# Cross-attention in fp32r pairs on one Trainium2 core: scores through a precomputed Wq_h^T K_h, and seven-product block multiplication for both large products

## The chip, the cores and the metric

The kernel runs on one core of a Trainium2 chip. The metric is the device time of one execution in microseconds. The engines have short names in the profile: PE is the matrix engine and PEld its weight load, DVE the vector engine, ACT the scalar engine, POOL the GpSimd engine, SP the engine that issues all DMAs here (SPq is its queue).

## The reference

The reference is one cross-attention layer, in fp32. B = 8 batches, T = 1024 rows of x, D = 1024, 16 heads of 64, and only S = 64 context rows in a batch.

```python
a = _layer_norm(audio_kv, ln_gamma, ln_beta)          # (8, 64, 1024)
Q = (hidden_states @ Wq.T)  ...  K = (a @ Wk.T)  ...  V = (a @ Wv.T)     # split in 16 heads
scores = jnp.einsum('bhtd,bhsd->bhts', Q, K) * scale
scores = jnp.where(mask, scores, -inf)
attn = jax.nn.softmax(scores, axis=-1)
out = jnp.einsum('bhts,bhsd->bhtd', attn, V)
out = out @ Wo.T                                       # heads side by side again
return hidden_states + jnp.tanh(gate) * out
```

The host only lays out the inputs (x also transposed, weights transposed).

## The kernel before

**Three products for one.** Every operand of a large product is held as two fp32r parts: hi is the operand copied to fp32r (ACT does it), lo is the operand minus hi (DVE or POOL does it). One block product is then three matmuls of 128x128 by 128x512 into one PSUM bank: lo by hi, hi by lo, hi by hi. These are lines L938, L939 and L940 (`product`), whatever the stage, so the three lines carry nearly all of PE's time.

**Stages.** The program has three stages, one after the other.

1. Context: layer norm of the 512 context rows (all batches), 32 transposes (L950), K and V for all batches: 64 block products each. K (scaled) and V (hi and lo) go to scratch tensors in DRAM.
2. Attention, `all_batches` over 8 batches of 16 units. A unit is one pair of heads (128 columns of Q) by 512 rows of x: 8 block products for Q (`q_part`), a copy of Q to SBUF (ACT, L703), the scores as plain fp32 matmuls against `k_diag` (`scores`, L1019; K of two heads on the diagonal of a 128x128 block, so that scores of two heads come out side by side), mask and maximum and shift (DVE), exponential (ACT, L727), row sums (DVE), normalising (POOL, L576), four transposes of the probabilities (`transpose_p`, L1031), their split (ACT L735, DVE L844), one block product against `v_diag` (`values`), and a copy (ACT, L743) that goes to `o_t_scratch` in DRAM. The stages of different units overlap by lags of 1 to 4 units; PE's order is first half of Q, scores of the unit before, second half of Q, values of three units before, transposes of two units before:

```python
all_batches(pe, [(q_first, 0), (scores, SCORES_LAG), (q_second, 0), (values, VALUES_LAG),
                 (transpose_p, TRANSPOSE_LAG)], lambda j: out_product(0, j))
```

3. Output product, 8 batches of 28 items. Here D by D times T is already cut in 2 x 2 blocks and done by seven products (Strassen's) instead of eight: for four groups of 256 rows, seven items each, an item being 4 x 3 matmuls. POOL forms the sums of blocks of the attention output (L610), ACT (L760) and DVE (L889) split them, DVE adds each finished item with factor tanh(gate) to one, two or three quarters of x in SBUF (L920), SP stores the result. The sums of Wo's blocks are made once.

Q's product (8 block products of 512 columns a unit) is done in full, with no such saving. All loads and stores are issued by SP in program order. The attention part of ACT, DVE and POOL is idle in stage 3, and nothing of stage 3 runs in stage 2, but for a few items at the seam.

The matmuls add up as follows. 128x512: 192 for K, 192 for V, 128 units x 24 for Q, 128 x 3 for values, 8 x 28 x 12 for the output, 6528 in all. 128x128: 512 fp32 score matmuls that the profile counts as two each (1024), and 512 + 32 transposes. That is the 8096 of the page.

## Time and profile before

| | |
|---|---|
| time, median of 3 runs | 1701.82 us (1701.62 to 1704.45) |
| span of the profiled execution | 1697.8 us |
| its own time beside the span | no time of its own is listed for it; the median lies 4.0 us above the span |
| PE busy | 1669.2 us, 98% |
| DVE, ACT, POOL busy | 931.4, 541.5, 608.3 us |
| granted clock of PE | 1.000 over the whole span (2.4 GHz) |
| DMA | 212.53 MB, 125 GB/s mean |

PE's "busy" is the union of its matmuls, whose modelled ends overlap; the distance from one start to the next says more than the duration of one. The page gives shares over the whole span; the windows below give them by stage.

### The profile page before, as it was taken

To read this page: it belongs to the slowest core of one execution; us is meant where nothing else is said; L and a number is where in the kernel's file an instruction comes from. 1 tells how busy PE (TensorE), PEld (TensorE's weight loads), DVE (VectorE), ACT (ScalarE), POOL (GpSimd) and SP (SyncE) were. 2 spreads that over 40 slices of the span, in tenths; PEclk is the share of its full clock that TensorE was granted. 3 is DMA by queue.
4 is the path that set the end of the run, shared out by engine and by line. 5 is a ranking of instruction groups with operands and counts; after the bars stand their busy time and mean duration, and the time that the engine had idled before them with its cause. 6 is when DMAs were issued, how large, how long until landed. Compare 5 with 4: busy or idle time off the path is not lost.

```text
span 1697.8 us, 23996 instructions
## 1 busy us (share of the span) xinstructions
PE 1669.2 (98%) x8096; PEld 1394.7 (82%) x8096; DVE 931.4 (55%) x1436; ACT 541.5 (32%) x942; POOL 608.3 (36%) x489
## 2 busy tenths in 40 slices
PE   6999999999999999999999999899999999999999
PEld 5878888888888888888888888678888888888887
DVE  6045644444444444444444444777666666666666
ACT  3243333333333333333333333522222222222221
POOL 6345632332332332332322323743333333333331
PEclk9999999999999999999999999999999999999999
DMA  5466442222222222222222221555444455445442
GB/s 200 163 239 212 161 141 78 80 76 73 79 75 74 83 71 74 82 73 74 86 69 76 80 67 63 180 195 191 160 148 148 175 179 189 150 167 178 149 149 100
DMA packets 117166, 212.53 MB, mean 125 GB/s; under 512 B 36480, under 2 KB 36608, under 8 KB 117120
## 3 DMA queue, kind: packets, MB, share of 16 engines
q1 hardware_dynamic: 117120, 211.93, 36.6%
q8 instruction: 27, 0.44, 0.1%
q14 instruction: 19, 0.16, 0.0%
HBM read 133.24 MB, written 78.64 MB: 125 GB/s over the span
## 4 chain that ended last, share of the span: by engine, by line
PE 95%; DVE 2%; DMA 2%; issue 1%; ACT 0%; POOL 0%; SPq 0%; DVEq 0%; ACTq 0%; POOLq 0%
PE banks L938 28%; PE banks L940 28%; PE banks L939 28%; PE banks L1019 7%; PE banks L1031 3%; DMA w_stage<-o_t_scratch 0%; DVE probs L920 0%; DMA o_t<-x 0%; DMA probs<-x 0%; DVE stats L800 0%; PE banks L950 0%; DVE act_in L793 0%; DMA out<-probs 0%; DVE o_t L920 0%; DMA act_in<-ctx_x 0%
## 5 line engine op out<-in xcount | busy, mean ns | idle before, releaser
L938 PE MATMUL banks<-act_hi,w_lo 128*128 128x512 f32 x1088 | 448.1, 412 | 1.5 <-DVE probs L838 1.5
L940 PE MATMUL banks<-act_hi,w_hi 128*128 128x512 f32 x1088 | 426.2, 392 | 0.0
L939 PE MATMUL banks<-act_lo,w_hi 128*128 128x512 f32 x1088 | 425.5, 391 | 0.0
L565 POOL TENSOR_TENSOR act_lo<-act_in,act_hi 128x512 fp32r<-128x512 f32 x128 | 164.9, 1290 | 601.3 <-ACT act_hi L657 601.3
L727 ACT ACTIVATE probs<-probs 128x512 f32<-128x512 f32 x128 | 80.9, 632 | 548.8 <-DVE probs L881 548.8
L869 DVE TENSOR_TENSOR probs<-banks,mask_bias 128x512 f32<-128x512 f32 x128 | 88.7, 693 | 286.1 <-PE banks L1019 286.1
L940 PEld LDWEIGHTS banks<-act_hi,w_hi 128*128 128x128 f32 x1088 | 204.5, 188 | 45.0
L938 PEld LDWEIGHTS banks<-act_hi,w_lo 128*128 128x128 f32 x1088 | 205.5, 189 | 36.6 <-DVE probs L838 1.9
L939 PEld LDWEIGHTS banks<-act_lo,w_hi 128*128 128x128 f32 x1088 | 205.8, 189 | 35.1
L760 ACT CAST act_hi<-block_sum 128x512 fp32r<-128x512 f32 x160 | 99.3, 620 | 333.2 <-POOL block_sum L610 173.4
L938 PE MATMUL banks<-w_hi,act_lo 128*128 128x512 f32 x512 | 199.7, 390 | 3.2 <-issue 3.2
L940 PE MATMUL banks<-w_hi,act_hi 128*128 128x512 f32 x512 | 199.3, 389 | 0.0
L939 PE MATMUL banks<-w_lo,act_hi 128*128 128x512 f32 x512 | 199.2, 389 | 0.0
L889 DVE TENSOR_TENSOR act_lo<-block_sum,act_hi 128x512 fp32r<-128x512 f32 x160 | 114.6, 716 | 123.4 <-ACT act_hi L760 123.4
L938 PE MATMUL banks<-act_hi,act_lo 128*128 128x512 f32 x448 | 174.7, 390 | 2.6 <-issue 1.6
L940 PE MATMUL banks<-act_hi 128*128 128x512 f32 x448 | 174.3, 389 | 0.0
L939 PE MATMUL banks<-act_lo,act_hi 128*128 128x512 f32 x448 | 174.3, 389 | 0.0
L610 POOL TENSOR_TENSOR block_sum<-w_stage 128x512 f32<-128x512 f32 x80 | 103.4, 1293 | 196.5 <-DVE act_lo L889 194.3
L610 POOL TENSOR_TENSOR block_sum<-act_in 128x512 f32<-128x512 f32 x80 | 104.6, 1309 | 175.0 <-DVE act_lo L889 175.0
L844 DVE TENSOR_TENSOR p_lo<-banks,p_hi 128x512 fp32r<-128x512 f32 x128 | 88.5, 692 | 112.9 <-ACT p_hi L735 112.9
L1019 PEld LDWEIGHTS banks<-k_diag,q_t 128*128 128x128 f32 x1024 | 133.8, 191 | 10.4 <-ACT q_t L703 0.5
L576 POOL TENSOR_TENSOR probs<-probs,row_rec 128x512 f32<-128x512 f32 x128 | 134.4, 1050 | 6.9 <-DVE row_rec L859 6.9
(77 smaller groups left out, 2238.4 us busy)
## 6 DMA issues: line engine op xcount, KB each, us to landing
act_in<-x_t SPq DMA_DIRECT2D x128, 256.0 KB, 3.1
o_t_scratch<-o_t SPq DMA_DIRECT2D x128, 256.0 KB, 3.1
probs<-x SPq DMA_DIRECT2D x32, 512.0 KB, 3.7
w_stage<-o_t_scratch SPq DMA_DIRECT2D x8, 2048.0 KB, 9.9
out<-probs SPq DMA_DIRECT2D x32, 512.0 KB, 3.4
act_in<-o_t_scratch SPq DMA_DIRECT2D x7, 2048.0 KB, 10.1
q_t<-x SPq DMA_DIRECT2D x16, 512.0 KB, 3.3
o_t<-x SPq DMA_DIRECT2D x16, 512.0 KB, 4.3
```

The costliest lines, as they stand in the source:

```text
L565: nc.gpsimd.tensor_tensor(act_lo[:, par, c, :], act_in[:, c, :], act_hi[:, par, c, :].bitcast(F32), ALU.subtract).then_inc(act_lo_made, 1)
L576: nc.gpsimd.tensor_tensor(pr, pr, rec, ALU.mult).then_inc(probs_done, 1)
L610: nc.gpsimd.tensor_tensor(o_sum[:, n % 2], o_part(g, one), o_part(g, other), ALU.add if sign > 0 else ALU.subtract).then_inc(part_summed, 1)
L727: nc.scalar.activation(probs[:, j % 4, :], probs[:, j % 4, :], ACT.Exp).then_inc(exp_done, 1)
L760: nc.scalar.copy(ring(k)[0], src).then_inc(part_hi_made, 1)
L844: nc.vector.tensor_tensor(p_lo[:, j % 2, :], banks[:, 4 + j % 2, :], p_hi[:, j % 2, :].bitcast(F32), ALU.subtract).then_inc(p_lo_made, 1)
L869: nc.vector.tensor_tensor(grouped(j), scores, bias, ALU.add).then_inc(masked, 1)
L889: nc.vector.tensor_tensor(lo, src, hi.bitcast(F32), ALU.subtract).then_inc(part_lo_made, 1)
L938: pe.matmul(to, wl, mh, start=first, stop=False)
L939: pe.matmul(to, wh, ml, start=False, stop=False)
L940: return pe.matmul(to, wh, mh, start=False, stop=last)
L1019: m = pe.matmul(banks[:, 2 + j % 2, cols], q_t[:, j % 2, cols], k_diag[:, p, :], start=True, stop=True)
```

## The change

The computation is reordered. For every batch and head, x Wq_h^T K_h^T = x (Wq_h^T K_h^T): a 1024 x 64 matrix for each head, so for each batch one 1024 x 1024 matrix M (16 heads side by side) is made once, and the scores of all heads are one product x M. Q, `q_t` and `k_diag` no longer exist.

1. **Context stage.** K as before, but all eight banks at once. Then 16 groups (`m_pair` by `v_tile`): a group makes M for all batches, for 128 rows of it and 8 heads, by 4 pairs x 6 matmuls whose contraction is 64 rows (a head), head 0 of a pair on partitions 0 to 63 and head 1 on 64 to 127, into different banks, one after the other in turn; in between come the matmuls of V (12 a group, two groups late). ACT and DVE copy M to one of three 2 MB buffers, SP stores it in DRAM (`store_m`: 1024 runs of 2 KB; batches are 4 MiB apart).
2. **Main stage: 224 steps in one pattern.** A round is 512 rows of x by the whole D, in seven products (steps) of 512 x 512 x 512, Winograd's form, where later products are added in PSUM to earlier ones. A step is two items (`item`, g = 0, 1) of 4 x 3 matmuls each. 16 rounds make the scores (16 x 7 = 112 steps), 16 rounds the output (112 steps). In a score round the first product starts with one more matmul for each g that adds the mask (L1079). For each step ACT and DVE split one block sum of the left operand (128x1024, `split_a_hi`, `split_a_lo`) into a ring of two, POOL makes 4 sums a round, and the results leave PSUM as 128x1024: 4 copies by ACT and 3 additions by DVE in a score round, 7 additions by DVE in an output round (`add_out`). The right operand (`parts`: seven block sums of M, hi and lo) is made anew for each batch, that is every 14 steps: 14 splits of 128x1024 on ACT and on DVE, 4 sums of 128x2048 on DVE. For the output it is made once, in 28 pieces, during steps 106 to 117.
3. **Attention beside it.** The scores go to DRAM and come back (256 KB a unit). Each unit (a pair of heads by 512 rows, 128 in all, 8 a round) passes seven stages, one half step apart each, one unit every 1.75 half steps, beginning half a round ahead of the output round that uses it: row maximum (DVE), exponential (ACT, now eight ACTIVATEs of 64 columns, since the shift is their bias; the mask addition and the shift on DVE are gone), row sum and reciprocal (DVE), normalising (POOL), transposes (PE), split (ACT, DVE), values (PE), copy into the x buffers (ACT; no trip through DRAM any more).

tanh(gate) is folded into V. The loops over batches are written out, with no branch. The residual x is loaded into the result buffer first, as before. Counts now: 128x512 matmuls 192 (K) + 384 (M) + 192 (V) + 2688 + 32 (scores and mask) + 2688 (output) + 384 (values) = 6560; transposes 512 + 32; fp32 score matmuls none. Of the 6560, the 384 for M use 64 of the 128 rows.

The core of the diff, PE first, then SP, then ACT and DVE (lines before: -, now: +):

```diff
-        def q_part(b, j, chunks):
...
-            for c in chunks:
-                if p == 0:
-                    pe.wait_ge(act_lo_made, n * NC + c + 1)
-                cols = slice(p * P, (p + 1) * P)
-                m = product(banks[:, j % 2, :], (w_hi[:, c, cols], w_lo[:, c, cols]),
-                            (act_hi[:, blk, c, :], act_lo[:, blk, c, :]), c == 0, c == NC - 1)
-        def scores(b, j):
...
-            for t in range(TPB):
-                cols = slice(t * P, (t + 1) * P)
-                m = pe.matmul(banks[:, 2 + j % 2, cols], q_t[:, j % 2, cols], k_diag[:, p, :],
-                              start=True, stop=True)
-            m.then_inc(scores_done, 1)
...
+        for i in range(GROUPS + V_LAG):
+            v = i - V_LAG
+            for half in range(2):
+                if i < GROUPS:
+                    for p in range(2 * half, 2 * half + 2):
+                        m_pair(i, p)
+                if v >= 0:
+                    for t in range(2 * half, 2 * half + 2):
+                        last = v_tile(v, t)
+            if v >= 0 and v % 2 == 1 and v % NC != NC - 1:
+                last.then_inc(v_used, 1)
...
+        def m_pair(i, p):
...
+                pe.wait_ge(m_copied_a, pair - 1)
+                pe.wait_ge(m_copied_b, pair - 1)
+            hp = 4 * hh + p
+            for t_w, t_k in ((1, 0), (0, 1), (0, 0)):
+                for h in range(2):
+                    rr = slice(h * HEAD, (h + 1) * HEAD)
+                    m = pe.matmul(banks[:, 2 * (p % 2) + h, :], w_ring[rr, w % 6, t_w, hp * P:(hp + 1) * P],
+                                  k_parts[rr, t_k, hp, :], start=t_w == 1, stop=t_w == 0 and t_k == 0)
+            m.then_inc(m_done, 1)
...
+        def store_m(i):
+            wait_group(i)
+            sp.dma_start(m_rows(i, 0, B), m_stage[i % 3][:]).then_inc(m_stored[i % 3], 16)
...
+        def item(s, g):
+            n, k = s // 7, s % 7
+            rnd = s // 14
+            if g == 0:
+                pe.wait_ge(a_lo_made, s + 1)
...
+            to = banks[:, 4 + g, :] if k in ON_F else banks[:, 2 * (n % 2) + g, :]
+            opens = k in ON_F[::2] or k == P1
+            if k == P1 and n < ROUNDS:
+                pe.matmul(to, ones_row[:], mask_mov[:].rearrange("p h s -> p (h s)"), start=True, stop=False,
+                          skip_group_check=True)
+                opens = False
+            for c in range(HC):
+                last = three(to, [a_ring[:, s % 2, t, c, g, :] for t in range(2)],
+                             [parts[:, k, t, c, :] for t in range(2)], opens and c == 0, c == HC - 1, True)
+            last.then_inc(item_done, 1)
...
+        for z in range(2 * STEPS):
+            item(z // 2, z % 2)
+            for u in units(z, VALUES):
+                values(u)
+            for u in units(z, TURN):
+                transpose_p(u)
...
+    MAX, EXP, SUM, TURN, SPLIT, VALUES, EVAC = 0, 1, 2, 3, 4, 5, 6
+    def unit_slot(u):
+        return 14 * (ROUNDS + u // 8 - 1) + 14 * (u % 8) // 8 - 7
...
+        def split_a_hi(s):
...
+            wait(act, item_done, 2 * (s - 1))
...
+            nc.scalar.copy(a_ring[:, s % 2, 0], a_source(n, k)).then_inc(a_hi_made, 1)
...
+        def exponential(u):
+            act.wait_ge(max_done, u + 1)
+            for g in range(8):
+                cols = slice(g * S, (g + 1) * S)
+                last = nc.scalar.activation(probs[:, u % 4, cols], probs[:, u % 4, cols], ACT.Exp,
+                                            bias=neg_max[:, u % 2, g:g + 1])
+            last.then_inc(exp_done, 1)
-            nc.scalar.activation(probs[:, j % 4, :], probs[:, j % 4, :], ACT.Exp).then_inc(exp_done, 1)
...
+        for s in range(STEPS):
+            if s + 1 < STEPS:
+                split_a_hi(s + 1)
+            if s > 0:
+                copy_out((s - 1) // 7, (s - 1) % 7)
+            if s < 104:
+                for rnd, q in refills(s):
+                    split_b_hi(rnd, q)
+            for z in (2 * s, 2 * s + 1):
+                for u in units(z, SPLIT):
+                    split_p_hi(u)
+                for u in units(z, EVAC):
+                    copy_o(u)
+                for u in units(z, EXP):
+                    exponential(u)
+            if s >= 104:
+                for rnd, q in refills(s):
+                    split_b_hi(rnd, q)
...
+        for s in range(STEPS):
+            rnd = s // 14 + 1
+            if s > 0:
+                add_out((s - 1) // 7, (s - 1) % 7)
+            if s + 1 < STEPS:
+                split_a_lo(s + 1)
+            if s < 104:
+                refill(s)
+            for z in (2 * s, 2 * s + 1):
+                for u in units(z, SUM):
+                    sum_rows(u)
+                for u in units(z, MAX):
+                    row_max(u)
+                for u in units(z, SPLIT):
+                    split_p_lo(u)
+            if s >= 104:
+                refill(s)
+            if s % 14 == 9 and rnd < B:
+                make_mask(rnd)
...
+        def add_out(n, k):
...
+            nc.vector.tensor_tensor(c_out[:, q], bank_pair(n, k), c_out[:, q], ALU.add).then_inc(added, 1)
+        def split_b_lo(rnd, q):
...
+            nc.vector.tensor_tensor(parts[:, k, 1, c:c + 2, :], b_raw[:, B_HOME[k], c:c + 2, :],
+                                    parts[:, k, 0, c:c + 2, :].bitcast(F32), ALU.subtract).then_inc(b_lo_made, 1)
```

What this does to the order of instructions, on the engines on which the prediction rests. First PE, at a unit's scores in the attention stage of the kernel before, and behind it the end of a unit:

```order
L939 MATMUL banks<-act_lo,w_hi 128x512
L940 MATMUL banks<-act_hi,w_hi 128x512
L1019 MATMUL banks<-k_diag,q_t 128x128 x4
L938 MATMUL banks<-act_hi,w_lo 128x512
L939 MATMUL banks<-act_lo,w_hi 128x512
```

The four fp32 matmuls L1019 stand between two halves of Q. In the changed kernel PE's order in an output round is this (12 matmuls of a step's item end with the first row; `p_parts` are the split probabilities, `a_ring` and `parts` the two operands of the step):

```order
L968 MATMUL banks<-parts,a_ring 128x512
L966 MATMUL banks<-p_parts,v_diag 128x512 [waits o_made,p_lo_made]
L967 MATMUL banks<-p_parts,v_diag 128x512
L968 MATMUL banks<-p_parts,v_diag 128x512
L1092 MATMUL banks<-ident,probs 128x128 [waits p_lo_made,probs_done]
L1092 MATMUL banks<-ident,probs 128x128 x3
L966 MATMUL banks<-parts,a_ring 128x512
```

No L1019 is left; values and transposes moved from between halves of Q to between items of the output product. Second, PE in a group of the context stage, where M and V alternate:

```order
L968 MATMUL banks<-w_ring,a_parts 128x512
L1002 MATMUL banks<-k_parts,w_ring 128x512 [waits m_copied_b,m_copied_a]
L1002 MATMUL banks<-k_parts,w_ring 128x512 x5
L1002 MATMUL banks<-k_parts,w_ring 128x512 [waits m_copied_b,m_copied_a]
L1002 MATMUL banks<-k_parts,w_ring 128x512 x5
L966 MATMUL banks<-w_ring,a_parts 128x512
```

These twelve L1002, two pairs, are new work; each pair waits for ACT's and DVE's copies of the pair two before it. Third, ACT: a unit in the kernel before, and then nearly a step and a half of an output round now.

```order
L703 COPY q_t<-banks 128x512
L735 CAST p_hi<-banks 128x512
L657 CAST act_hi<-act_in 128x512
L743 COPY o_t<-banks 128x512
L727 ACTIVATE probs<-probs 128x512
```

```order
L697 ACTIVATE probs<-probs,neg_max 128x64 x8
L656 CAST a_ring<-xq 128x1024
L706 CAST p_parts<-banks 128x512
L714 COPY xq<-banks 128x512
L697 ACTIVATE probs<-probs,neg_max 128x64 x8
L656 CAST a_ring<-a_sum 128x1024
```

The copy of Q is gone, the exponential is in eight pieces, and the split of the next step's operand (L656) now stands behind attention work on the same engine.

## Rows read from the trace of the kernel before

**Rows 1.** The page, part 1: busy time, share of the span, instructions

```profile
PE 1669.2 (98%) x8096; PEld 1394.7 (82%) x8096; DVE 931.4 (55%) x1436; ACT 541.5 (32%) x942; POOL 608.3 (36%) x489
```

**Rows 2.** The page, part 4: shares of the chain that ended last

```profile
PE 95%; DVE 2%; DMA 2%; issue 1%; ACT 0%; POOL 0%; SPq 0%; DVEq 0%; ACTq 0%; POOLq 0%
```

**Rows 3.** Windows: us, busy by engine (instructions), PE clock, DMA share, GB/s

```profile
600.00:1050.00 450.00, 450.00 (x2340) 380.68 (x2338) 213.35 (x360) 164.44 (x300) 137.13 (x120) 1.00 0.24 76
1050.00:1080.00 30.00, 27.02 (x138) 21.66 (x137) 17.24 (x28) 11.44 (x22) 12.40 (x11) 1.00 0.21 71
1080.00:1120.00 40.00, 35.20 (x149) 27.05 (x148) 35.09 (x38) 20.02 (x36) 34.38 (x24) 1.00 0.58 198
```

**Rows 4.** Timeline of PE in the output stage, matmuls 27 places apart: start, us

```profile
1499.80 0.39 PE L938 MATMUL banks<-act_hi,act_lo 128*128 128x512 f32 x1
...
1505.92 0.39 PE L938 MATMUL banks<-act_hi,act_lo 128*128 128x512 f32 x1
```

**Rows 5.** The chain in order of time, attention stage: start, us, one unit's scores

```profile
275.82 0.89 PE banks L1019 x8
```

**Rows 6.** Timeline of PE at the start: context transposes, then K's first product

```profile
16.35 3.04 PE L950 MATMUL banks<-ident,act_in 128*128 128x128 f32 x13 [2.88 <-DVE act_in L793]
19.28 0.76 PE L938 MATMUL banks<-act_hi,w_lo 128*128 128x512 f32 x1
```

**Rows 7.** The chain at the end: last matmul, last addition

```profile
1694.21 0.24 PE banks L940
1694.48 0.75 DVE o_t L920
```

**Rows 8.** DMA issues: tensors, count, KB each, median us to landing

```profile
out<-probs SPq DMA_DIRECT2D x32, 512.0 KB, 3.4
act_in<-o_t_scratch SPq DMA_DIRECT2D x7, 2048.0 KB, 10.1
```

**Rows 9.** Windows with the DMA engines near full

```profile
75.00:80.00 5.00, 5.00 (x24) 4.14 (x23) 0.00 (x0) 0.14 (x1) 0.53 (x1) 1.00 1.04 409
...
95.00:100.00 5.00, 5.00 (x24) 4.14 (x23) 2.71 (x4) 3.15 (x3) 0.00 (x0) 1.00 0.95 354
```

**Rows 10.** Groups by line and shape: busy us, mean ns, idle before

```profile
L654 ACT CAST w_hi<-w_stage 128x1024 fp32r<-128x1024 f32 x16 | 16.6, 1049 | 20.9 <-DMA w_stage<-wk_t 15.2 <-DMA w_stage<-wq_t 5.7
L813 DVE TENSOR_TENSOR w_lo<-w_stage,w_hi 128x1024 fp32r<-128x1024 f32 x8 | 11.0, 1391 | 54.6 <-ACT w_hi L654 54.6
L920 DVE SCALAR_TENSOR_TENSOR probs<-banks,tanh_gate,probs 128x512 f32<-128x512 f32 x160 | 114.9, 743 | 7.9 <-DMA probs<-x 7.9
L853 DVE TENSOR_REDUCE row_sum<-probs 128x8 f32<-128x512 f32 x128 | 87.8, 686 | 88.6 <-ACT probs L727 88.6
L859 DVE RECIPROCAL row_rec<-row_sum 128x8 f32<-128x8 f32 x128 | 24.7, 193 | 0.0
L844 DVE TENSOR_TENSOR p_lo<-banks,p_hi 128x512 fp32r<-128x512 f32 x128 | 88.5, 692 | 112.9 <-ACT p_hi L735 112.9
L735 ACT CAST p_hi<-banks 128x512 fp32r<-128x512 f32 x128 | 75.2, 587 | 62.6 <-PE banks L1031 62.6
L727 ACT ACTIVATE probs<-probs 128x512 f32<-128x512 f32 x128 | 80.9, 632 | 548.8 <-DVE probs L881 548.8
L662 ACT ACTIVATE tanh_gate<-gate_s 128x1 f32<-128x1 f32 x1 | 0.2, 198 | 0.0
L610 POOL TENSOR_TENSOR block_sum<-act_in 128x512 f32<-128x512 f32 x80 | 104.6, 1309 | 175.0 <-DVE act_lo L889 175.0
L576 POOL TENSOR_TENSOR probs<-probs,row_rec 128x512 f32<-128x512 f32 x128 | 134.4, 1050 | 6.9 <-DVE row_rec L859 6.9
```

**Rows 11.** Timeline of DVE: the shortest kind of split, and the longest

```profile
1080.90 0.69 DVE L889 TENSOR_TENSOR act_lo<-block_sum,act_hi 128x512 fp32r<-128x512 f32 x1 [0.32 <-ACT act_hi L760]
...
1086.19 1.77 DVE L889 TENSOR_TENSOR act_lo<-act_in,act_hi 128x512 fp32r<-128x512 f32 x1
```

**Rows 12.** The page, part 3: the queue that brings instructions: packets, MB, share

```profile
q8 instruction: 27, 0.44, 0.1%
```

1473 lines of the change are left out of this document (752 added, 721 removed), and 7 rows, old and new, of the table PRODUCTS.

## Prediction

> **What bounds the kernel now.** I read the page first. PE is busy for 98% of the span [rows 1], and the chain that ended last is PE's own work for 95% [rows 2], so the time is PE's work laid end to end, and the change has to be priced on PE. The busy time of the other engines is not in the sum as long as each stays below PE stage by stage; that is the second question. The clock needs no term: the windows show it at 1.00, the upper of its two levels, 2.4 GHz, with PE working without a break [rows 3].
>
> The price of a matmul I take from starts, not from durations (0.39 us, which overlap). In the output stage 27 matmuls of 128x512 start within 1505.92 - 1499.80 = 6.12 us, so one costs 0.2267 us [rows 4]. In the attention stage 2340 instructions fill 450 us without idle time [rows 3]. A unit has 27 of 128x512, 8 score passes and 4 transposes, 39 in all, so there are 60 units and one takes 7.50 us. 27 x 0.2267 = 6.12 leaves 1.38, of which 0.89 are the scores [rows 5] and 0.49 the four transposes and the seams.
>
> I test this on the kernel before: 19.3 to the first product of K [rows 6], 6528 x 0.2267 = 1479.9, 128 x 1.38 = 176.6, the other 16 context transposes 1.8, PE's idle time at the change of stage 3.0 + 4.8 [rows 3], 3.6 from the start of the last matmul to the end [rows 7]. Together 1689, 9 us under the span of 1697.8 (0.5%). So the method is good to half a per cent, and errs low.
>
> **The change, part by part.**
>
> *Start.* The first product of K now comes behind all 32 context transposes instead of behind 16. Thirteen took 3.04 us at the start, 0.23 each [rows 6]; 16 more cost 3.7: 23.0.
>
> *K.* 192 x 0.2267 = 43.5, as before.
>
> *M and V.* 576 matmuls; one after the other that is 130.6. Two things can move it. M's 384 work on 64 of the 128 rows, neighbours on different halves. No row of before shows such matmuls. From above each costs a full 0.2267 (the streamed columns are the same 512); from below two neighbours share one slot, 192 slots fewer, 43.5 us less, 87.1 for the stage. But the stage also moves about 45 MB: 33.6 MB of M, 6 of weights, the rest V, sums of Wo, first blocks of x. With the DMA engines full the rows show 409 and 354 GB/s [rows 9], so 110 to 127 us whatever PE does. So a gain on PE is mostly taken back by the stores of M. I take 125, from DMA's slower full rate, a little under PE's serial 131; ends 110 and 162 (the latter is 16 stores of 2 MB one after the other at the 10.1 of the only 2048 KB row [rows 8]).
>
> The Trainium skill ("TensorE: Matmul & The Clock Gate", Part 3, Packing small matmuls) says that small matmuls whose operands lie in different row groups run side by side, 3.07 times as fast for four of 32 rows. By it the 87.1 would be PE's own bound; no run so far shows it. My sum stays at 125 by the DMA rows either way.
>
> *Scores.* 112 steps x 24 + 32 mask matmuls = 2720 x 0.2267 = 616.6. In the place of this stood Q (3072) and the fp32 scores: here the change gives 352 x 0.2267 + 128 x 0.89 = 194 us, of which M takes back 87 at its serial price. That difference is nearly the whole gain: seven products instead of eight on D x D, and no fp32 passes.
>
> *Output and attention.* 2688 + 384 = 3072 x 0.2267 = 696.4, and 128 x 0.49 = 62.7 for transposes: 759.1. PE's count here is unchanged; only its neighbours are new.
>
> *Are the other engines hidden?* A batch of scores (14 steps) takes PE 340 x 0.2267 = 77.1. ACT has 28 splits and 8 copies of 128x1024 at 1.05: 37.8. DVE has 28 splits at 1.39, 4 sums twice that size, 6 additions at 2 x 0.743: 38.9 + 11.1 + 8.9 = 58.9 (76%). POOL has 8 sums at 2 x 1.31: 21 [rows 10]. An output round (7 steps) takes PE 168 x 0.2267 + 8 x (0.68 + 0.49) = 47.5. DVE: 7 x (1.49 + 1.39) + 8 x (0.686 + 0.686 + 0.193 + 0.692) = 38.2 (80%). POOL 10.5 + 8.4 = 19. ACT: 7 x 1.05 + 8 x (0.587 for each of the two PSUM copies) + 64 short exponentials at e each = 16.7 + 64 e. The rows have 0.198 for one column and 0.632 for 512; 64 columns on the line between are 0.25, so 32.7 (69%) [rows 10]. All hidden, at nothing, and if the cover went: ACT alone would set the round above e = 0.48.
>
> The latency also fits. The operand of step s + 1 may be split when product s - 1 is done (ring of two). In a score step ACT needs 1.05 and then DVE 1.39; DVE may first have an addition of 1.49, beside ACT. That is 2.9 of 5.44 us. In an output step the two splits come first in the loop, and attention's waits stand behind them, so PE gets a late operand only if an engine falls behind by over 3 us. What presses on DVE is POOL: a 128x512 split takes 0.69, and 1.77 at worst [rows 11]. POOL is busy 27% to 40% of the time here, so I add nothing in steady state.
>
> *Two seams.* Between context and scores DVE owes a copy of M, two splits of M's first block sum, a sum of 2.8 and the first operand, 0.7 + 2.8 + 2.8 + 1.4 = 7.7, behind 1.05 of ACT, 8.7 in all, against 5.4 of PE (24 matmuls of V): 3.3 late. In steps 0, 1 and 4 DVE has three splits and a sum, 6.95 against 5.44, 4.5 more; less what other steps absorb: 7 in all. In steps 106 to 117 the 28 pieces of Wo add 28 x 0.69 = 19.3 to DVE, 1.6 a step, so 7.1 against 6.8, four us late, and SP's loads of pieces wait for splits: 5.
>
> *End.* The last addition is 128x1024, 1.5, and a 512 KB store 3.4 [rows 8, 10]: 5.
>
> Sum: 23.0 + 43.5 + 125 + 616.6 + 759.1 + 7 + 5 + 5 = 1584, and 5 for what the same method left out above (half of the 9, since one seam of two is new work already counted): 1589. The median stood 4.0 over the profiled span before, so **1593**.
>
> **The rivals.**
>
> *M goes side by side and its stores keep up.* For it: the windows at 409 GB/s. Against it: those are short and mostly loads, and here SP must first wait for each group's copies. The stage takes 110, and the first seam vanishes in part: 1593 - 15 - 7 = 1571 to 1578. 17%.
>
> *A helper or a store sets the pace somewhere.* Either M's stores run one after the other (162 instead of 125: 1630), or ACT and DVE, with attention's waits between their splits in strict order, hold each of 112 output steps up by 0.3: 1627. For it: DVE at 80% with a split that can take 2.5 times its price. Against it: three buffers for M, and three us of slack. 18%.
>
> *Slower: M's stores.* A store writes 2 KB runs to eight places 4 MiB apart, as no store before does. If that ran at half the rate of the 2048 KB row, 20.2 a group, the stage would take 323 instead of 125: 1791. It decides above (125 + 109) / 16 = 14.6 us a store. Against it: neighbouring partitions lie 4 KB apart, as in the loads of that row. 4%. The skill ("DMA: Bandwidth & Descriptors", Latency and other measured facts) speaks against the change here: it gives 103 GB/s for copies whose partitions lie 4 MiB apart against 214 with padding, by which 2.1 MB would take 20 us; its case has that distance between partitions, ours between runs of one partition.
>
> *Slower: eight short exponentials.* If 64 columns cost nearly what 512 do, 0.632, ACT's round is 57.1 against 47.5, 16 x 9.6 = 154 late: 1747. It decides above e = 0.59. 1%.
>
> That the change has no effect would need new stalls of just 109 us, 1%; loops written out mean more code to load, but 27 packets bring half a megabyte now [rows 12], and the products of V, straight code too, run without a gap [rows 9].
>
> **How the numbers follow.** Forecast 59%: 1593, its own range 1578 to 1612. The rivals 17, 18, 4, 1 and 1%. Low end 1567 takes in the first rival; high end 1633 both forms of the second; outside are the slower cases and the tails, some 17%. A change of 0.2% (3.4 us) is about what can be told from none. Faster 94%, same 1%, slower 5%.
>
> **What would show it.** No fp32 matmul; PE's distance 0.227 in all stages; 5.4 to 5.5 us from step to step in the scores, 6.8 in the output; PE busy above 96%. M's pairs: two starts within a few ns would mean side by side, then DMA near full for 110 us and PE waiting for copies that wait for stores. The 64-column ACTIVATE near 0.25. I am wrong if PE waits for `a_lo_made` in most output steps, or if a 2 MB store lands over 14 us after its issue.

## The result, and the profile after

The changed kernel takes 1643.08 us (median of 4 runs, 1641.88 to 1643.65), beside 1701.72 for the kernel before on the same chip: 58.6 us less; the ratio is 0.9648, 95% interval 0.9636 to 0.9660 (the two medians alone give 0.9655). The prediction was 1593.0 with 1567 to 1633 as its range: the direction was right, the gain was half of what was forecast, and the time lies 10 us above the range. The profiled execution has a span of 1640.1, so the time to explain is 1640.1 against the sum of 1589. One execution of e6 below took 5479.87 us, which nothing on record explains; it is a slow run and left out of e6's time.

The page of the changed kernel, parts 1, 4 and 6 (they answer to [rows 1, 2, 8]):

```profile
PE 1554.1 (95%) x7104; PEld 1254.7 (77%) x7104; DVE 1173.1 (72%) x1216; ACT 860.6 (52%) x1822; POOL 536.4 (33%) x294
...
PE 69%; DVE 14%; issue 6%; DMA 6%; ACT 4%; POOL 0%; SPq 0%; ACTq 0%; DVEq 0%; POOLq 0%
...
m_scratch<-m_stage SPq DMA_DIRECT2D x14, 2048.0 KB, 15.6
```

The count of matmuls is the forecast one. But the chain is no longer one engine's: of 95% PE it has become 69%, and DVE holds 14%. A chain of that kind says that PE waits now and then, and the windows say where: M and V, the first seam (the change from one stage to the next, with its first round), score rounds, second seam, output rounds (columns as in [rows 3]).

```profile
63.00:180.00 117.00, 105.06 (x578) 69.61 (x576) 49.47 (x74) 53.34 (x85) 33.79 (x15) 0.97 1.02 353
180.00:290.00 110.00, 92.66 (x368) 74.26 (x368) 87.86 (x57) 47.81 (x51) 31.07 (x11) 0.89 0.56 190
290.00:768.00 478.00, 460.86 (x2015) 376.45 (x2014) 366.93 (x233) 209.88 (x213) 138.28 (x47) 1.00 0.46 157
768.00:932.00 164.00, 144.83 (x643) 117.03 (x642) 118.22 (x147) 107.94 (x261) 50.44 (x32) 0.96 0.53 164
932.00:1595.00 663.00, 660.26 (x3106) 542.56 (x3105) 486.83 (x631) 416.43 (x1182) 247.89 (x166) 1.00 0.43 135
```

PE's order is known, so the starts of its matmuls give the length of each of the 224 steps. This table is worked out from them (us; a step of 24 matmuls at the price of [rows 4] is 5.44, the first of a score round 5.89, an output round 47.5, a score round with attention beside it 47.9):

```
round  step 0     1     2     3     4     5     6    sum
  0     14.84  8.15  5.61  9.25  8.31  5.44  5.44   57.0
  7      5.89  5.44  5.46  5.57  7.19  5.58  5.44   40.6
  8      5.89  5.44  5.44  5.44  6.79  5.59  5.44   40.0
 14      5.89  5.44  5.44  5.44  5.44  8.47  7.28   43.4
 15      7.07  6.60 13.87  8.32  6.61  7.05  8.24   57.8
 16     11.37  7.29 12.09  7.43  6.61  9.91  7.26   62.0
 19      6.61  6.60  7.11  6.61  6.59  6.97  7.28   47.8
```

Against the prediction's sum, term by term:

| Term | Predicted | Measured |
|---|---|---|
| Start to K's first product | 23.0 | 19.6 |
| K | 43.5 | 43.7 |
| M and V | 125 | 116.3 (63.35 to 179.63) |
| First seam (gap before step 0 and round 0, over 38.5) | 7 | 25.3 |
| Score rounds 1 to 13, over 38.5 each | 0 | 23.6 |
| Rounds 14 to 16 (163.1), over 38.5 + 2.8 + 47.9 + 47.5 | 5 | 26.4 |
| Rounds 17 to 31 (704.1), over 699.5 | 0 | 4.6 |
| Last matmul to the end | 5 | 5.0 |

The 2.8 are what attention already gives PE in round 14: three units' transposes and two units' values. The differences add up to 18.3 + 23.6 + 21.4 + 4.6 - 3.4 - 8.7 + 0.2 = 56.0; the sum of 1589 held 5 for what the method leaves out, and 51.0 are left of the 51.1 by which the span is over it. Three places hold nearly all of the loss, each about a third.

**The score rounds.** One step of nearly each round is late. DVE beside that step, in an odd round (start, us; the step that begins at 434.19 has the late operand, and the table books the wait to the step before it, so DVE's row that ends there is the one to start from, and one reads upwards):

```profile
413.71 4.13 DVE L862 TENSOR_TENSOR parts<-b_raw,parts 128x1024 fp32r<-128x1024 f32 x2 [0.63 <-ACT parts L680]
417.94 2.29 DVE L883 TENSOR_TENSOR b_raw<-b_raw 128x2048 f32<-128x2048 f32 x1
...
421.41 1.23 DVE L862 TENSOR_TENSOR parts<-b_raw,parts 128x1024 fp32r<-128x1024 f32 x1
422.55 2.64 DVE L844 TENSOR_SCALAR mask_mov<-mask_u 1x512 fp32r<-1x512 uint8 x1
...
426.25 1.21 DVE L862 TENSOR_TENSOR parts<-b_raw,parts 128x1024 fp32r<-128x1024 f32 x1
427.57 4.31 DVE L883 TENSOR_TENSOR b_raw<-b_raw 128x2048 f32<-128x2048 f32 x1
431.80 1.21 DVE L905 TENSOR_TENSOR c_out<-banks,c_out 128x1024 f32<-128x1024 f32 x1
432.93 1.21 DVE L849 TENSOR_TENSOR a_ring<-xq,a_ring 128x1024 fp32r<-128x1024 f32 x1
...
443.07 2.35 DVE L862 TENSOR_TENSOR parts<-b_raw,parts 128x1024 fp32r<-128x1024 f32 x2
```

POOL in the same stretch, and PE's late step:

```profile
413.22 2.40 POOL L552 TENSOR_TENSOR a_sum<-xq 128x1024 f32<-128x1024 f32 x1 [3.51 <-DVE a_ring L849]
421.54 3.37 POOL L552 TENSOR_TENSOR a_sum<-xq 128x1024 f32<-128x1024 f32 x1 [5.92 <-DVE a_ring L849]
426.47 3.26 POOL L552 TENSOR_TENSOR a_sum<-a_sum,xq 128x1024 f32<-128x1024 f32 x1 [1.55 <-DVE a_ring L849]
```

```profile
434.19 0.50 PE L966 MATMUL banks<-parts,a_ring 128*128 128x512 f32 x1 [1.58 <-DVE a_ring L849]
```

The same work has two prices. The 128x2048 sum takes 2.29 us at 417.94, with POOL idle, and 4.31 at 427.57, beside POOL's sum of 426.47. Two splits take 2.35 at 443.07 and 4.13 at 413.71, beside POOL's of 413.22. The mask row, one partition of 512, takes 2.64, and 0.41 where POOL is idle. In three steps DVE loses 2.0 + 1.8 + 2.2 = 6 us, and PE's step is 1.75 late (7.19 for 5.44).

The rows show how the price comes about: of two such instructions the one that starts second waits until the first has ended. POOL's sum that starts at 421.54 finds DVE's split of 421.41 at work; the split keeps its 1.23, and POOL's sum, 2.40 where it starts alone, takes 3.37 and ends 2.27 after the split. DVE's mask row then starts at 422.55 in the middle of POOL's sum, which ends at 424.91, and itself ends 0.28 behind it. In the same way POOL's sum of 426.47 waits for DVE's split of 426.25, and DVE's sum of 427.57 waits for POOL's, which ends at 429.73, and ends 2.15 later. This holds for all of DVE's instructions of these kinds between 290 and 768 us: those that start within a sum of POOL's end 1.08 (split), 2.15 (sum) or 0.28 us (mask row) after it, within 0.01, and those that start before POOL's take their short time.

**The first seam** is a chain of transfers. In order of time:

```profile
161.15 15.54 DMA m_scratch<-m_stage
...
176.71 13.95 DMA xq<-x_t
...
190.78 2.39 POOL a_sum L552
...
193.19 1.06 ACT a_ring L656
...
194.28 2.46 DVE a_ring L849
...
201.24 0.77 PE banks L966
202.01 0.43 PE banks L967
```

The second half of x has its place in a buffer that M's stage holds, so its load waits for a store, and then shares the DMA engines with the next stores. Between the last two pieces shown the chain has 4.51 us of "issue". DVE's rows have work there, the two splits of M's block sum that this step needs too, and the granted clock follows:

```profile
196.65 4.49 DVE L862 TENSOR_TENSOR parts<-b_raw,parts 128x1024 fp32r<-128x1024 f32 x2
...
218.14 6.00 DVE L862 TENSOR_TENSOR parts<-b_raw,parts 128x1024 fp32r<-128x1024 f32 x2 [0.63 <-ACT parts L680]
```

```profile
201.30:206.00 4.70, 4.70 (x11) 3.71 (x12) 4.65 (x4) 3.00 (x3) 1.18 (x1) 0.50 0.65 235
```

Both pairs take 2.35 with POOL idle, and PE starts 0.1 us after each of them ends: 2.1 and 3.65 us of this seam are contention with POOL as well. The matmuls after the gap are 0.43 apart, with a granted clock of 0.50: PE's clock had fallen to the lower of its two levels, 1.2 GHz, during the idle time before them. By the starts, three waits (6.8 before step 0, 5.9 before step 1, 3.7 before step 4) and 35 matmuls at the lower clock behind them, 7 us, are 23 of the 25.3.

**The second seam** has two waits. ACT and DVE in step 106, where four pieces of Wo are split with three buffers:

```profile
828.96 0.62 ACT L670 CAST parts<-wo_piece_ab 128x512 fp32r<-128x512 f32 x1 [4.01 <-DMA wo_piece_ab<-wo_t]
```

```profile
824.84 4.00 DVE L857 TENSOR_TENSOR parts<-wo_piece_ab,parts 128x512 fp32r<-128x512 f32 x2
...
847.20 1.28 DVE L857 TENSOR_TENSOR parts<-wo_piece_ab,parts 128x512 fp32r<-128x512 f32 x2
```

The fourth piece can only be loaded when the first is split (4.01 us of waiting). And two splits take 4.00 at 824.84, with POOL's normalising of 824.44 and its sum of 825.44 beside them, but 1.28 at 847.20.

### The profile page after: what moved, and what is told of

It is laid out like the page before. It is cut to its first block, busy times and chain, and to the rows that moved or that the text cites. A ratio compares the mean times of both kernels' runs of the same rounds, so it can differ in the third digit from the quotient of the medians.

```text
span 1640.1 us, 19978 instructions
## 1 busy us (share of the span) xinstructions
PE 1554.1 (95%) x7104; PEld 1254.7 (77%) x7104; DVE 1173.1 (72%) x1216; ACT 860.6 (52%) x1822; POOL 536.4 (33%) x294
## 4 chain that ended last, share of the span: by engine, by line
PE 69%; DVE 14%; issue 6%; DMA 6%; ACT 4%; POOL 0%; SPq 0%; ACTq 0%; DVEq 0%; POOLq 0%
PE banks L966 22%; PE banks L968 21%; PE banks L967 21%; DVE a_ring L849 4%; DVE parts L862 3%; PE banks L1092 3%; DVE c_out L905 2%; DMA w_raw<-wq_b 2%; ACT parts L680 1%; PE banks L1002 1%; DMA w_raw<-wv_t 1%; ACT c_out L691 1%; DMA m_scratch<-m_stage 1%; DVE mask_mov L844 1%; DVE b_raw L883 1%
## 5 line engine op out<-in xcount | busy, mean ns | idle before, releaser
L966 PE MATMUL banks<-parts,a_ring 128*128 128x512 f32 x1792 | 717.6, 400 | 30.7 <-DVE a_ring L849 18.2
L968 PE MATMUL banks<-parts,a_ring 128*128 128x512 f32 x1792 | 703.4, 393 | 0.0
L967 PE MATMUL banks<-parts,a_ring 128*128 128x512 f32 x1792 | 702.8, 392 | 0.0
L966 PEld LDWEIGHTS banks<-parts,a_ring 128*128 128x128 f32 x1792 | 339.7, 190 | 106.0 <-DVE a_ring L849 25.2
L968 PEld LDWEIGHTS banks<-parts,a_ring 128*128 128x128 f32 x1792 | 339.1, 189 | 73.5
L967 PEld LDWEIGHTS banks<-parts,a_ring 128*128 128x128 f32 x1792 | 339.9, 190 | 67.2
L697 ACT ACTIVATE probs<-probs,neg_max 128x64 f32<-128x64 f32 x1024 | 259.1, 341 | 49.2 <-DVE neg_max L910 49.2
L905 DVE TENSOR_TENSOR c_out<-banks,c_out 128x1024 f32<-128x1024 f32 x160 | 195.1, 1219 | 119.0 <-PE banks L968 114.4
L849 DVE TENSOR_TENSOR a_ring<-a_sum,a_ring 128x1024 fp32r<-128x1024 f32 x128 | 188.4, 1472 | 113.7 <-ACT a_ring L656 112.5
L656 ACT CAST a_ring<-a_sum 128x1024 fp32r<-128x1024 f32 x128 | 134.0, 1047 | 211.6 <-PE banks L968 202.3
L552 POOL TENSOR_TENSOR a_sum<-xq 128x1024 f32<-128x1024 f32 x64 | 167.8, 2622 | 210.0 <-DMA xq<-x_t 105.1
L862 DVE TENSOR_TENSOR parts<-b_raw,parts 128x1024 fp32r<-128x1024 f32 x112 | 186.1, 1676 | 29.4 <-ACT parts L680 29.0
L656 ACT CAST a_ring<-xq 128x1024 fp32r<-128x1024 f32 x96 | 100.5, 1046 | 159.6 <-PE banks L968 159.6
L680 ACT CAST parts<-b_raw 128x1024 fp32r<-128x1024 f32 x112 | 115.2, 1047 | 60.2 <-DVE b_raw L883 54.4
L849 DVE TENSOR_TENSOR a_ring<-xq,a_ring 128x1024 fp32r<-128x1024 f32 x96 | 123.9, 1291 | 2.4 <-ACT a_ring L656 2.4
## 6 DMA issues: line engine op xcount, KB each, us to landing
m_scratch<-m_stage SPq DMA_DIRECT2D x14, 2048.0 KB, 15.6
```

The source lines that it names most:

```text
L552: nc.gpsimd.tensor_tensor(a_sum[:, A_SUM[k]], one, two, op).then_inc(sum_made, 1)
L656: nc.scalar.copy(a_ring[:, s % 2, 0], a_source(n, k)).then_inc(a_hi_made, 1)
L680: nc.scalar.copy(parts[:, k, 0, c:c + 2, :], b_raw[:, B_HOME[k], c:c + 2, :]).then_inc(b_hi_made, 1)
L697: last = nc.scalar.activation(probs[:, u % 4, cols], probs[:, u % 4, cols], ACT.Exp, bias=neg_max[:, u % 2, g:g + 1])
L849: nc.vector.tensor_tensor(a_ring[:, s % 2, 1], a_source(n, k), a_ring[:, s % 2, 0].bitcast(F32), ALU.subtract).then_inc(a_lo_made, 1)
L862: nc.vector.tensor_tensor(parts[:, k, 1, c:c + 2, :], b_raw[:, B_HOME[k], c:c + 2, :], parts[:, k, 0, c:c + 2, :].bitcast(F32), ALU.subtra ...
```

## The experiments

Unless said otherwise each is the changed kernel with one edit; times are medians, with the ratio to the kernel before (1702.1 to 1702.8 beside these runs) and its interval.

**e1: DVE's order.** In the score steps the split of the next operand comes before the addition.

```diff
-                if s > 0:
+                if s > 0 and s >= 112:
                     add_out((s - 1) // 7, (s - 1) % 7)
                 if s + 1 < STEPS:
                     split_a_lo(s + 1)
+                if 0 < s < 112:
+                    add_out((s - 1) // 7, (s - 1) % 7)
```

> Edit: in the 112 score steps DVE splits the next operand before it adds the finished product to the result, not after. First theory (DVE runs late at the fifth step of a round, P7, because an addition of 1.2 us and a block sum stand ahead of the split that PE waits for): that step goes from 7.19 and 6.79 us to about 6.0 and 5.6, 14 rounds x 1.2 = 17 us, so about 1626. Rival (the late operand comes from ACT or from POOL's sum, or PE waits for the addition itself): the step stays at 7.2 and 6.8, or another step takes over the delay, 1643.

1654.69, ratio 0.9719 [0.9703, 0.9735]: 12 us slower. The late step of the even rounds is 8.01 instead of 6.79. Its rows on DVE:

```profile
391.51 4.27 DVE L883 TENSOR_TENSOR b_raw<-b_raw 128x2048 f32<-128x2048 f32 x1
395.71 3.43 DVE L849 TENSOR_TENSOR a_ring<-xq,a_ring 128x1024 fp32r<-128x1024 f32 x1
399.06 1.21 DVE L905 TENSOR_TENSOR c_out<-banks,c_out 128x1024 f32<-128x1024 f32 x1
```

In the changed kernel, in the same round, the addition comes first, beside this sum of POOL's:

```profile
390.12 1.21 DVE L905 TENSOR_TENSOR c_out<-banks,c_out 128x1024 f32<-128x1024 f32 x1
391.25 2.30 DVE L849 TENSOR_TENSOR a_ring<-xq,a_ring 128x1024 fp32r<-128x1024 f32 x1
```

```profile
388.13 4.34 POOL L552 TENSOR_TENSOR a_sum<-a_sum,xq 128x1024 f32<-128x1024 f32 x1
```

The addition, one of whose operands is in PSUM, takes 1.21 beside POOL, and only what is then left of POOL's sum falls on the split. In e1 the split, both operands in SBUF, waits out POOL's sum by itself (3.43), the addition runs after it, and PE waits 2.41 for the addition. So the order before the edit had put the work that POOL does not touch beside POOL. The theory that order alone was at fault fell.

**e2: POOL's sums made small.** After round 0 the sums take 4 of 128 columns (this leaves most of the block sums out).

```diff
-                nc.gpsimd.tensor_tensor(a_sum[:, A_SUM[k]], one, two, op).then_inc(sum_made, 1)
+                w = 4 if n > 0 else P
+                nc.gpsimd.tensor_tensor(a_sum[:, A_SUM[k], :, :, 0:w], one[:, :, :, 0:w], two[:, :, :, 0:w], op
+                                        ).then_inc(sum_made, 1)
```

> Edit: POOL's sums of blocks of the left operand cover 4 of 128 columns in every round but the first (so most of these sums is left out); all waits, splits and products stay. Theory (DVE's two-input work in SBUF nearly stands still while POOL's works, which is why the 128x2048 sum takes 4.3 instead of 2.3 us and the mask row 2.6): L883 falls to 2.3 in all calls, the mask row to 0.4, the fifth step of a round to 5.44, 14 x 1.6 = 23 us in the score rounds and some in the second seam, about 1612. Rival (DVE simply has too much work ahead of the split): L883 shortens little, the step stays above 6.5, above 1635.

1604.88, ratio 0.9430 [0.9415, 0.9446]. Every step of score rounds 1 to 13 is 5.44 (5.89 the first): 38.5 a round, as the sum had it. DVE's groups in the score rounds (lines are 2 further down here) are all at their short price:

```profile
L885 DVE TENSOR_TENSOR b_raw<-b_raw 128x2048 f32<-128x2048 f32 x24 | 55.0, 2291 | 2.4 <-DVE parts L864 0.5
L846 DVE TENSOR_SCALAR mask_mov<-mask_u 1x512 fp32r<-1x512 uint8 x6 | 2.8, 470 | 0.0
```

That was 76.6 us with a mean of 3190 ns, and 13.6 with 2261, in the changed kernel. So the loss in the score rounds goes with POOL's sums. Small sums are also ready sooner for ACT; e6 and e12, in which they come later and the loss goes too, rule that out as the cause. The output rounds take 47.4 instead of 47.8, so what they lose goes with the sums as well. But the second seam stayed, 56.6 + 58.3 for rounds 15 and 16 where it was 57.8 + 62.0.

**e3: an eighth of M stored** (the other seven batches are left out, and all rounds read the first).

```diff
-                sp.dma_start(m_rows(i, 0, B), m_stage[i % 3][:]).then_inc(m_stored[i % 3], 16)
+                sp.dma_start(m_rows(i, 0, 1), m_stage[i % 3][:, 0:1]).then_inc(m_stored[i % 3], 16)
```

> Edit: only one batch of M in eight is stored (256 KB instead of 2 MB a group), and all rounds read that one; so 7/8 of the stores of M are left out, everything else stays. Theory (the stage of M and V and the start of the scores are set by the stores of M, the DMA engines being full): the stage falls from 116 to 90 to 97 us (PE's own 87 plus waits for copies), and the delay at the first steps from 25 us to under 8; together about -40, 1603. Rival (PE waits for the copies of M by ACT and DVE, or DVE's own work makes the first steps late): the stage stays above 110 and the first round at 50 us or more, above 1630.

1625.53, ratio 0.9546 [0.9530, 0.9562]. With the DMA engines half idle the stage still takes 109.0 (116.3 before):

```profile
63.00:172.00 109.00, 104.31 (x577) 69.24 (x576) 54.23 (x76) 57.50 (x89) 37.27 (x17) 0.97 0.49 160
```

So the stores cost the stage 7 us, and PE with what it waits for the rest. They cost more behind it: round 0 fell from 57.0 to 47.8.

**e4: head by head.** A pair's three matmuls for head 0 (rows 0 to 63), then three for head 1.

```diff
-                for t_w, t_k in ((1, 0), (0, 1), (0, 0)):
-                    for h in range(2):
+                for h in range(2):
+                    for t_w, t_k in ((1, 0), (0, 1), (0, 0)):
```

> Edit: in a pair of M the three matmuls of head 0 come first and then the three of head 1, so that neighbours use the same 64 rows, instead of taking turns. Theory (matmuls on different halves of the rows run side by side, and the stage is held by its stores, so only what exceeds them costs): twelve of them take 2.7 to 3.0 instead of 1.66 us, PE's work in the stage becomes 131, the stage goes from 116 to about 131, 1658. Rival (a matmul of 64 rows is short by itself): 1.66 us again and 1643. If the stores did not hold the stage, it would be +43, 1686.

1646.39, ratio 0.9666 [0.9650, 0.9682]: no change in the stage (116.9). Twelve matmuls take the same time in both orders. This did not decide between side by side and short by itself, which needed e9.

**e5: a fourth buffer for pieces of Wo.**

```diff
-        wo_piece_in = sems("wo_piece_in", 3)
+        NP = 4
+        wo_piece_in = sems("wo_piece_in", NP)
...
-            return wo_piece_c[:, :] if pc % 3 == 2 else wo_piece_ab[:, pc % 3, :]
+            if pc % NP >= 3:
+                return wo_piece_de[:, pc % NP - 3, :]
+            return wo_piece_c[:, :] if pc % NP == 2 else wo_piece_ab[:, pc % NP, :]
```

> A fourth 2 KB slot for the pieces of Wo, so that a step that holds four pieces has no round trip of a load inside it. Theory (at the second seam the splits wait for pieces that SP may load only when a slot comes free): the two waits of ACT for pieces, 4.0 and 2.6 us, and their echo go, rounds 15 and 16 fall from 57.8 + 62.0 to some 110, the time from 1643 to 1633. Rival (the seam is DVE's own load, and its work beside POOL's): ACT waits less, DVE ends no sooner, within 2 us of 1643.

1641.38, ratio 0.9635 [0.9612, 0.9657]: not to be told from no change. Rounds 15 and 16 are 53.8 + 61.5.

**e6: POOL waits for DVE.** The first sum for the next round waits for DVE's sum of B.

```diff
+                    if 0 < n < ROUNDS:
+                        pool.wait_ge(t_made, 4 * (n // 2) + (2 if n % 2 == 0 else 4))
                     one, two, op = a_quad(n, 1, 0), a_quad(n, 1, 1), ALU.add
```

> POOL's first sum of the next round waits until DVE has made the sum of B in that stretch (two of four sums of a round are moved past the 128x2048 subtraction of DVE). All work stays. Theory (DVE's SBUF work is drawn out while POOL works, and that sets the late step): L883 falls from 4.3 to 2.3 us, the late step of a score round from 7.19 and 6.79 to 5.5 to 5.8, 14 rounds by 1.4 each: 1643 - 20 = 1623. Rival 1 (DVE has too much in these three steps whatever POOL does): the late step stays above 6.8, 1640. Rival 2 (the sums now come late for ACT): a stall at the second or third step of each round, 1643 or more.

1628.46, ratio 0.9556 [0.9531, 0.9580], 14.6 less with all work kept. Odd rounds 38.7, even ones 39.7. DVE's groups:

```profile
L851 DVE TENSOR_TENSOR a_ring<-xq,a_ring 128x1024 fp32r<-128x1024 f32 x36 | 60.3, 1675 | 0.0
...
L885 DVE TENSOR_TENSOR b_raw<-b_raw 128x2048 f32<-128x2048 f32 x24 | 54.9, 2289 | 2.4 <-DVE parts L864 0.5
```

The sum is at its short price, and the splits of the operand pay instead (1675 ns, 1361 before): the contention was moved to work that had slack, not removed.

**e7: the mask row three steps later.**

```diff
-                if s % 14 == 9 and rnd < B:
+                if s % 14 == 12 and rnd < B:
```

> Only DVE's mask row is moved, from the third step of an odd score round (where DVE is behind) to the sixth. Theory: the row of one partition costs 2.6 us only beside POOL and 0.4 elsewhere, and the late step of the 7 odd rounds falls by the whole 1.75 that it was over 5.44: 1643 - 12 = 1631. Rival (other work of DVE, the 4.3 us sum, would still be late by itself): 7.19 falls to no less than 6.8 and the time by 3: 1640.

1640.41, ratio 0.9625 [0.9604, 0.9647]. The row now takes 407 ns, and the late step of the odd rounds is 6.83 instead of 7.19: the rival's number. But DVE does not lose less. The split that now stands in the row's place meets the same sum of POOL's (the rows of e7):

```profile
422.24 3.26 DVE L849 TENSOR_TENSOR a_ring<-a_sum,a_ring 128x1024 fp32r<-128x1024 f32 x1
```

```profile
421.05 3.36 POOL L552 TENSOR_TENSOR a_sum<-xq 128x1024 f32<-128x1024 f32 x1 [5.92 <-DVE a_ring L849]
```

It takes 3.26 where it took 1.20. So the 2.2 us were a wait for POOL that falls on whatever DVE starts there, and the edit saved only the row's own 0.4. That the sum of 4.3 us would be late by itself, as the rival has it, this run does not show.

**e8: e5, e6 and e7 together.**

> The three edits together: fourth slot, POOL's sums after DVE's sum of B, mask row three steps later. All work and all results stay. If each of the three causes is its own: 1643 - 10 - 20 = 1613 (the mask row's share is in the 20), score rounds at 38.9 to 39.3. If the causes only pass the lateness on to each other, above 1625.

1627.04, ratio 0.9557 [0.9539, 0.9575]: what e6 gave. Score rounds 38.8 and 39.8; the seams are as they were (rounds 15 and 16: 56.2 + 62.6). The edits pass the lateness on to each other, as the second expectation had it.

**e9: all products of M on one half of the rows** (the second head of each pair is left out), and **e10: on all 128 rows** (the two heads are mixed).

```diff
-                        rr = slice(h * HEAD, (h + 1) * HEAD)
+                        rr = slice(0, HEAD)        # e9; slice(0, P) in e10
```

> All products of M take their operands from rows 0 to 63; none works on rows 64 to 127. This leaves out the second head of each pair. Theory A (neighbours on different halves of the rows work side by side, within or across the pairs of three): with one half only, each product costs the full 0.2267 us, a group 36 x 0.2267 = 8.2 instead of 6.35 us, the stage 16 x 1.8 = 29 longer, the time from 1643 to 1672. Theory B (a product over 64 rows is short by itself, whichever half): twelve still take 1.66 us, the time stays within 3 of 1643.

> All products of M take all 128 rows, which mixes the two heads (the result is not M). Theories A and B both: nothing is side by side and nothing is short, 0.2267 each, a group 8.2 us, the stage 16 x 1.8 = 29 longer, 1672. If the stage stays at 117, the number of rows has no part in it, and the stage was never bound by PE at 0.2267 per product.

e9: 1667.32, ratio 0.9793 [0.9773, 0.9812], the stage 146.2; the time rises by 24 where the stage rises by 30, since the gap before step 0 shrinks from 6.8 to 0.9. e10: 1656.29, ratio 0.9728 [0.9711, 0.9746], the stage 133.7. PE in the changed kernel and in e9, twelve products of M and the first of V behind them:

```profile
101.65 1.67 PE L1002 MATMUL banks<-k_parts,w_ring 64*128 64x512 f32 x12
103.25 0.50 PE L966 MATMUL banks<-w_ring,a_parts 128*128 128x512 f32 x1
...
104.84 1.66 PE L1002 MATMUL banks<-k_parts,w_ring 64*128 64x512 f32 x12
```

```profile
101.67 3.03 PE L1002 MATMUL banks<-k_parts,w_ring 64*128 64x512 f32 x12
104.63 0.50 PE L966 MATMUL banks<-w_ring,a_parts 128*128 128x512 f32 x1
```

From the start of the twelve to the start behind them: 1.60 with two halves, 2.96 with one. A matmul over 64 rows is not short by itself; two on different halves run side by side. The single starts in the trace say it directly: in the changed kernel they come in twos 1 to 11 ns apart, and the twos are 0.23 apart; in e9 every one is 0.23 behind the last. In e4 they also come in twos (some 10 ns apart), though the program has three of the same half in a row. Kept to that order, only three neighbours in twelve lie on different halves, and the twelve would take nine slots, 2.04 us (an estimate from the 0.2267); they take 1.60. So PE does not seem to keep to the program's order there. The Trainium skill ("TensorE: Matmul & The Clock Gate", Part 3, Packing small matmuls) says that small matmuls in different row groups run concurrently; under "Why this matters for your kernels" it says that one of 32 rows alone takes as long as a full one. The runs agree in both, for 64 rows. The Trainium skill says in Part 3 of that page as well that matmuls start and end strictly in order; e4's starts, and the time of its twelve, are against that.

e10 shows a second price. Its twelve matmuls of M and six of V repeat every 4.08 us, which is 18 x 0.2267 exactly:

```profile
99.91 2.88 PE L1002 MATMUL banks<-k_parts,w_ring 128*128 128x512 f32 x12
...
103.99 2.88 PE L1002 MATMUL banks<-k_parts,w_ring 128*128 128x512 f32 x12
```

In e9 the same eighteen take 4.55 and in the changed kernel 3.19, where 12 x 0.2267 would be 2.72: 0.47 over in both. The single starts place it: the step from one kind to the other and the one behind it are 0.32 to 0.33 where 0.23 is normal. So going from 64 rows to 128 and back costs 0.47 us here.

**e11: e8 with the pieces of Wo spread** as 2 or 3 a step, where two steps had 4.

```diff
+            pieces = [(B, pc) for pc in range(28) if 106 + 3 * pc // 7 == s]
```

> The kernel with three edits, and the 28 pieces of Wo spread over the twelve steps as 2 or 3 a step, where two steps had 4. Theory (a step with four splits of 0.7 us, drawn out to 4 us for a pair beside POOL, holds back DVE's split of the transposed probabilities, for which PE waits; then PE's clock falls): rounds 15 and 16 fall from 56.2 + 62.6 to some 104, the time from 1627 to 1612. Rival (the pieces' lateness comes from SP's loads or from attention's own start): less than 5 us.

1625.82, ratio 0.9551 [0.9536, 0.9565]: 1 us under e8, the rival's side.

**e12: e11, and the sums that follow an even round wait for DVE's last split of B.**

```diff
-                        pool.wait_ge(t_made, 4 * (n // 2) + (2 if n % 2 == 0 else 4))
+                        if n % 2 == 0:
+                            pool.wait_ge(t_made, 4 * (n // 2) + 2)
+                        else:
+                            pool.wait_ge(b_lo_made, 14 * (n // 2) + 14)
```

> As the kernel before, and POOL's sums that follow an even score round wait until DVE has made that batch's last split of B. Theory (what is left of 39.7 against 38.5 in the even rounds is DVE's a_ring at 2.6 and parts at 3.4 us beside these two sums): even rounds 38.7, 7 x 1.0 = 7 less than the kernel before, 1605 if that comes to 1612. Rival: the sums now come too late and the second or third step of the odd rounds stalls: the same or slower than the kernel before.

1613.79, ratio 0.9488 [0.9470, 0.9506], 12 under e11 and 29 under the changed kernel: the fastest that does all the work. Even rounds 38.7, odd 38.8, round 0 51.5 instead of 56.9. What is left over 38.5 in 13 rounds is 3 us.

**e13: both causes of the second seam out at once** (e2's small sums, four buffers, spread pieces; most of the sums are left out).

> Fourth slot, pieces spread as 2 or 3 a step, and POOL's sums of A cut to 4 of 128 columns after round 0 (this leaves most of the sums out). Theory (the round trip of a piece's load and DVE's work drawn out beside POOL cover each other): rounds 15 and 16 fall from 56.6 + 58.3 to 100 to 104, the time from 1605 to 1592. Rival (a third cause, the start of attention): both rounds stay above 110 in sum, 1602 or more.

1595.51, ratio 0.9373 [0.9359, 0.9387]. Rounds 15 and 16: 51.6 + 54.3 = 105.9. They were 119.8 in the changed kernel, 114.9 with the sums alone out (e2), 115.3 with the buffer alone (e5) and 115.0 with buffer and spread pieces, the sums kept (e11, which has the edits of e6 and e7 too). The two causes cover each other: either alone gives 5 at most, both give 14.

**e14: e12, and POOL's sums in the second seam wait until that step's pieces are split.**

```diff
+                split_now = max([pc + 1 for pc in range(28) if 106 + 3 * pc // 7 <= s], default=0)
+                if split_now and n in (15, 16) and k in (P5, P6, P4):
+                    pool.wait_ge(b_lo_made, 14 * B + split_now)
```

> The fastest kernel so far (1613.8), and in the two rounds of the second seam POOL's sums wait until DVE has split that step's pieces of Wo. All work stays. Theory (contention with POOL is what is left of the seam once the pieces' loads are no round trip): the pairs of splits of 3.7 to 4.5 us go to 1.3, rounds 15 and 16 from 116 to 104, the time to 1602. Rival (the sums come too late for ACT, or attention's start sets the seam): 1610 to 1616.

1632.34, ratio 0.9584 [0.9571, 0.9597]: 18.6 slower than e12. ACT waits for the sum that was moved:

```profile
819.73 1.04 ACT L673 CAST a_ring<-a_sum 128x1024 fp32r<-128x1024 f32 x1 [3.34 <-POOL a_sum L562]
```

Step 3 of rounds 15 and 16 takes 14.07 and 13.53. The outcome is the rival's (sums too late), and worse than its number. This place for POOL's sums costs more than it saves; that the seam's contention could be scheduled away is not shown, and other places were not tried.

**e15: fewer changes between 64 and 128 rows:** a group's 24 products of M in one run, then its 12 of V.

> The changed kernel, with the 24 products of M of a group in one run and then its 12 of V, where they stood as 12, 6, 12, 6. Theory (each pair of changes between 64 and 128 rows costs 0.47 us and PE sets the stage): 16 x 0.47 = 7.5 less, less what PE waits for the copies of M's banks, 0.1 to 0.3 a group: the stage 117 to 111 to 113, the time 1643 to 1638. Rival (the stores of M set the stage, DMA share 1.02): stage and time within 2 us of before.

1642.60, ratio 0.9649 [0.9635, 0.9664]: no change. PE from 80 to 160 us:

```profile
L1002 PE MATMUL banks<-k_parts,w_ring 64*128 64x512 f32 x260 | 36.5, 409 | 10.5 <-ACT m_stage L625 9.0 <-DVE m_stage L826 1.5
```

PE waits 10.5 us for the copies of M's banks in these 80 us, where it was 4.7: with 24 in a run there is no V to cover the copy. The 5.6 us for which V's products waited for DVE are gone there. Over the whole stage PE waits 16.5 us where it was 12.0, and the stage takes 118.5 where it was 116.3. So the saving of 0.47 a group, if it is there, went into waits; this run can't show it.

## Why the prediction was wrong, by its own steps

**The step that failed** is "POOL is busy 27% to 40% of the time here, so I add nothing in steady state". It came two sentences after the row that had the price: a split of 0.69 us that takes 1.77 [rows 11]. I read that as a rare case and put the term at nothing. Two things were wrong. The price is no factor on DVE's work: a split, a sum or a mask row that starts while POOL's sum is at work waits for its end, up to 2.2 us each time; a sum of 2.29 becomes 4.31, a mask row of 0.41 becomes 2.64. And what counts is not the mean over a batch but three steps in a row. DVE's mean load is nearly what I had: 366.93 us in 478, 77%, against 76%. My prices for its work were 14 to 23% too high (1.39 for a split that takes 1.22, 0.743 x 2 for an addition that takes 1.21), and the contention filled just that gap. The condition "PE gets a late operand only if an engine falls behind by over 3 us" was right, and it was met: DVE lost 6 in three steps. e2 (the loss gone), e6 and e12 (the loss nearly gone with all work kept) show this cause; 23.6 us in the score rounds, 4.6 in the output rounds, and a part of each seam. In e12 DVE's splits of x still wait for POOL (mean 1751 ns, 1361 in the changed kernel), but where they have slack.

The Trainium skill ("GPSIMD Engine Reference", Specifications) says that GpSimd's SBUF interfaces are shared with VectorE, with contention for instructions that have two SBUF inputs or run in a two-port mode. The rows agree: the split and the sum (two SBUF inputs) wait for POOL's sum to end, the addition with an operand in PSUM takes 1.21 in either case. The prediction drew on rules on matmuls and on stores and not on this one, which spoke against the change's move of sums of 128x2048 to DVE beside POOL.

**"Two seams ... 7 in all".** 25.3 were measured. The chain that I worked out (M's copy, splits, sum, operand on DVE) is there, but what sets the time is one that I left out: a store of 15.5 us, then a load of x of 14.0 that may start only when the store has freed its buffer. e3 takes the transfers away: the gap and round 0 become 5.1 + 47.8 instead of 6.8 + 57.0, 11 of the 25 us. e12 takes the later contention away: 51.5 for round 0, 5.5 less. No run takes both, and they may overlap, since in e3 the late steps of the end of round 0 (9.25 and 8.31) are already 6.78 and 5.54. The remainder I did not separate; it holds the lower clock behind three waits (0.43 between matmuls, 13, 10 and 12 of them, 2.0 to 2.6 us each time), and DVE's own chain.

**"In steps 106 to 117 ... four us late, and SP's loads of pieces wait for splits: 5".** 26.4 were measured. Both mechanisms named were right, and both too small by far, since I had not counted that with four pieces a step and three buffers a load lies inside the step (4.01 us), nor POOL (4.00 for 1.28). Together they are worth 14 (e13). The other 12.6 stay with both out. In e13 they lie in step 5 of round 14 (8.47, 2.0 over), where attention starts, in steps 3, 5 and 6 of round 15 (8.33, 7.65, 8.24) and in steps 1, 2, 3 and 5 of round 16 (7.55, 8.86, 7.43, 9.91). No run tests what they are. For the longest, 9.9 in every run, the rows name a cause: the last two pieces of Wo are split in the step before PE needs them, and on ACT behind eight exponentials (ACT, then DVE):

```profile
920.00 2.02 ACT L697 ACTIVATE probs<-probs,neg_max 128x64 f32<-128x64 f32 x8 [0.84 <-DVE neg_max L910]
921.93 0.60 ACT L670 CAST parts<-wo_piece_c 128x512 fp32r<-128x512 f32 x1
...
923.17 0.68 DVE L857 TENSOR_TENSOR parts<-wo_piece_ab,parts 128x512 fp32r<-128x512 f32 x1
```

PE waits 2.9 us there and starts at 923.96, 0.11 after DVE's last split.

**M and V.** 125 was forecast and 116.3 measured, with the wrong limit. I took the time from the DMA engines' rate. They were full (share 1.02, 353 GB/s), but e3 shows that without most of the stores the stage would take 109.0. The lower bound of PE, 87.1, rests on pairs that do start side by side (e9): it is what PE's slots add up to. To it come the changes of 0.47, twice a group in 14 groups, 13 us, and waits for copies; 9 us in e3 are then left, of which 4.7 are waits in the rows; the other 4 I did not place. So the first rival ("M goes side by side and its stores keep up") described this stage rightly in its mechanism, and its gain was used up by what it had not in it.

**The start.** 23.0 was forecast for the first product of K and 19.6 measured: the 16 added transposes fill time in which PE had stood idle for DVE before (2.88 us in [rows 6], 0.78 in the changed kernel).

**What held.** The distance of 0.2267 in all stages; 5.44 from step to step wherever nothing waits; output rounds 47.8 against 47.5 (the rest is POOL's sums, by e2); the eight short exponentials at 2.02 us a unit, 0.25 each, as interpolated; the last 5 us; no sign of a cost of the written-out code. The second rival had "ACT and DVE ... in strict order, hold each of 112 output steps up by 0.3": it did not come, an output round of seven steps loses 0.3 in all. The stores of M landed in 15.6 us, above the 14.6 at which my slower rival was to decide and above the 14 that I had given as a sign of being wrong, and yet cost 7 us in the stage: most follow each other by 6.3 to 8.7 us, so two or three were under way at a time, and the time of one says nothing on their pace. That bound was worked out as if they ran one by one, and was wrong.

## What to carry to other kernels

When work with two SBUF operands is moved to DVE, or made larger there, list what POOL does at that time, step by step and not as a mean, and ask of each meeting which starts first: the second waits for the first one's end, however short it is itself. Put DVE's work on PSUM beside POOL, or let POOL start later, if its result has slack; and follow what the edit puts in the old place, for the wait falls on that (e7). Where two causes sit in the same place, take both out before saying that neither matters. And at a change of stage, follow each buffer that changes its owner: a load behind a store stood ahead of the operand that came 6 us late here, where the whole seam had been put at 7.

## What the runs showed of the hardware

- DVE beside POOL: a split or a block sum with two SBUF operands on DVE, or the mask row, and a sum on POOL do not run together; the one that starts second waits for the end of the first. 128x2048 takes 2.29 us alone and 4.27 to 4.31 when it starts within POOL's sum; two splits of 128x1024 2.35 and 4.13; a row of one partition with 512 uint8 0.41 and 2.64; an addition with a PSUM operand 1.21 and a row sum or maximum of 128x512 0.67 to 0.69 in both cases. A split that starts before POOL's sum keeps its 1.2. POOL's sum takes 2.40 when it starts first, 3.3 to 3.4 behind a split, and 4.34 behind a sum of 128x2048.
- PE over 64 rows: neighbours on different halves start within some ns of each other and cost 0.113 us each, on the same half 0.227. They find each other also when the program has three of one half in a row. A change from 64-row to 128-row matmuls and back costs 0.47 us.
- Behind the three waits of 3.7 to 6.8 us in the first seam 10 to 13 of PE's matmuls are 0.43 apart (granted clock 0.50, 1.2 GHz) and then 0.23 again: 2.0 to 2.6 us more than the wait itself. Behind the waits of 1.6 to 2.7 us in the score rounds there is no such run.
